# Reordering the start and the last products of an adaLN transformer block: second batch's statistics first, GpSimd held back, sums in pairs, row pairs at the end

## The reference, cut to what matters

```python
mod = (silu(c) @ wmod).reshape(2, 6, 1, 512)          # sa, ca, ga, sb, cb, gb
h = layernorm(x) * (1 + ca) + sa                      # x: (2, 512, 512)
q, k, v = h @ wq, h @ wk, h @ wv                      # 32 query heads, 8 key/value heads of 128
q = q * cos + rotate_half(q) * sin                    # the same for k
att = softmax(where(tril, q @ k.T / sqrt(128), -inf))
x = x + ga * ((att @ v) @ wo)                         # ga, gb: sign kept, size at least 0.25
h = layernorm(x) * (1 + cb) + sb
x12 = h @ w12.T + b12; x1, x2 = split(x12, 2)
x = x + gb * ((silu(x1) * x2) @ w3.T + b3)
```

## Time and profile before

| | us |
|---|---|
| median of 3 runs (795.09 to 797.32) | 795.21 |
| the profiled execution, its own time | 795.66 |
| its span in the profile | 793.9 |

### The profile page before, as it was taken

One profiled execution on the slowest core, in us unless ns is written; L12 is line 12 of the kernel. 1 busy time (PEld: TensorE's weight loads), 2 busy tenths in 40 slices (PEclk: granted clock), 3 DMA queues, 4 the chain that ended last, 5 costly groups with the idle time before them and its releaser, 6 DMA issues.

```text
span 793.9 us, 11522 instructions
## 1 busy us (share of the span) xinstructions
PE 765.9 (96%) x3526; PEld 623.4 (79%) x3526; DVE 604.0 (76%) x1296; ACT 507.3 (64%) x1201; POOL 567.8 (72%) x384
## 2 busy tenths in 40 slices
PE   7999999999999999999999999999999998889997
PEld 2755788887888788887888888888888877667885
DVE  5777878777877787778778786868787788459685
ACT  2466775776676766786677666767677765865331
POOL 2545885879587957795779677898768998447453
PEclk9999999999999999999999999999999999999999
DMA  9625646874867576867776767866677855989011
GB/s 314 232 66 143 204 132 186 193 248 117 238 154 234 157 218 154 219 185 199 182 212 190 192 186 189 251 158 211 145 228 188 280 146 170 272 264 248 1 54 53
DMA packets 189781, 147.13 MB, mean 185 GB/s; under 512 B 60564, under 2 KB 166164, under 8 KB 187672
## 3 DMA queue, kind: packets, MB, share of 16 engines
q1 hardware_dynamic: 189304, 146.33, 65.1%
q10 hardware_dynamic: 416, 0.07, 0.0%
HBM read 91.82 MB, written 54.53 MB: 184 GB/s over the span
## 4 chain that ended last, share of the span: by engine, by line
PE 50%; POOL 22%; DVE 11%; ACT 10%; issue 4%; DMA 3%; SPq 1%; DVEq 0%; ACTq 0%; POOLq 0%
PE q_bank L511 12%; PE out_bank L599 11%; POOL pT_lo L1412 7%; PE o_bank L576 7%; PE x_bank L511 7%; PE s_bank L511 5%; POOL rope_tmp L1438 4%; ACT probs L1185 3%; POOL qT L1412 3%; POOL wo_lo_sb L1412 3%; ACT probs L1193 2%; POOL wq_lo_sb L1412 2%; PE s_bank L798 1%; PE s_bank L785 1%; DVE x_y L1134 1%
## 5 line engine op out<-in xcount | busy, mean ns | idle before, releaser
L1412 POOL TENSOR_TENSOR pT_lo<-pT_raw,pT_hi 128x1024 fp32r<-128x1024 f32 (+1 forms) x96 | 194.2, 2038 | 60.1 <-ACT pT_hi L1162 60.1
L1185 ACT ACTIVATE probs<-probs,neg_max 128x32 f32<-128x32 f32 (+15 forms) x256 | 130.6, 512 | 144.8 <-DVE neg_max L860 144.8
L1412 POOL TENSOR_TENSOR qT<-rope_tmp,qT 128x512 fp32r<-128x512 f32 x64 | 83.7, 1308 | 85.4 <-ACT qT L1162 85.4
L878 DVE STREAM_TRANSPOSE turned<-probs 128x512 f32<-128x512 f32 (+1 forms) x64 | 96.7, 1511 | 36.3 <-DMA spread_dram<-turned 28.3
L1438 POOL TENSOR_TENSOR rope_tmp<-rope_tmp 128x512 f32<-128x512 f32 x80 | 110.4, 1388 | 13.2 <-DVE rope_tmp L825 9.4
L1193 ACT ACTIVATE probs<-probs,row_inv 128x32 f32<-128x32 f32 (+15 forms) x256 | 111.9, 508 | 1.8 <-DVE row_inv L868 1.8
L511 PE MATMUL s_bank<-k_both,qT 128*128 128x416 f32 (+11 forms) x576 | 100.6, 324 | 2.0 <-DVE neg_max L860 2.0
L511 PE MATMUL q_bank<-hT_hi,wq_hi_sb 128*128 128x512 f32 x244 | 97.2, 399 | 5.1 <-DVE rope_tmp L825 5.1
L860 DVE CUSTOM_DVE_ANT_0 probs<-s_bank,mask_sb 128x416 f32<-128x416 f32 (+2 forms) x192 | 87.0, 501 | 15.9 <-PE s_bank L511 15.7
L511 PEld LDWEIGHTS s_bank<-k_both,qT 128*128 128x128 f32 x576 | 90.4, 191 | 9.9 <-DVE neg_max L860 2.6
L599 PE MATMUL out_bank<-wo_hi_sb,attn_hi 128*128 128x512 f32 x248 | 97.0, 391 | 1.2 <-DVE attn_lo L882 1.2
(11 more groups left out here) (267 smaller groups left out, 1673.2 us busy)
## 6 DMA issues: line engine op xcount, KB each, us to landing
spread_dram<-turned SPq DMA_DIRECT2D x64, 256.0 KB, 3.8
pT_raw<-spread_dram SPq DMA_DIRECT2D x16, 1024.0 KB, 5.8
spread_dram<-turned SPq DMA_DIRECT2D x64, 192.0 KB, 4.0
pT_raw<-spread_dram SPq DMA_DIRECT2D x16, 768.0 KB, 4.9
wq_raw<-in_L_attn_wq_dram SPq DMA_DIRECT2D x36, 256.0 KB, 4.2
wo_raw<-in_L_attn_wo_dram SPq DMA_DIRECT2D x9, 1024.0 KB, 5.4
spread_dram<-turned SPq DMA_DIRECT2D x64, 128.0 KB, 4.4
pT_raw<-spread_dram SPq DMA_DIRECT2D x16, 512.0 KB, 5.5
```

The lines of the kernel that those rows point to most:

```text
L878: nc.vector.transpose(dst, src).then_inc(blocks_turned, 1)
L1185: nc.scalar.activation(rows, rows, ACT.Exp, bias=neg_max[:, par, t:t + 1], scale=-1.0, accum_out=row_sum[:, par, t:t + 1]).then_inc(exp_do ...
L1412: nc.gpsimd.tensor_tensor(dst, src, hi.bitcast(f32), ALU.subtract).then_inc(done, 1)
```

## The change

Five edits, all of order or of waits; no instruction is added to or taken from the arithmetic.

1. DVE: the statistics of batch 1 (four `bn_stats` and `norm_scale(1, 2)`) stand ahead of the five first rotations. Before, they stood between them.
2. POOL: the low part of the key weights waits until batch 0 is normalised (`x_normed[0]`), the low parts of query heads 0 and 1 until DVE has made the low parts of `hT` of batch 0 (`h_lo[0]`), those of heads 2 and 3 until `norm_scale` of batch 1 is through (`norm_ready` 2). The low part of the value weights comes after the second query head's rotation.
3. POOL: the sums of the query rotations come in pairs (sum, sum, low, low) instead of one by one.
4. PE and ACT: `modulation_rows(3)` moves up to the place of `project_v(0)`, into bank `s_banks[3]`, and `project_v(0)` moves behind `turn_x(1)`; ACT's copies and high parts are put in the matching order.
5. PE: the last products take rows 0 and 1 through part 2 and part 3 first, then rows 2 and 3.

```diff
-        mod_banks = [q_bank, out_bank, out_bank, q_bank, out_bank, x_bank]
+        mod_banks = [q_bank, out_bank, out_bank, s_banks[3], q_bank, x_bank]
 ...
+                        pe.wait_ge(roped, 5)
                         project_q(out_bank[:, :], 1, 0, h_lo[1])
 ...
+                    if b == 1 and k == KC - 1:
+                        pe.wait_ge(mod_rows_copied, 3)
 ...
             project_q(out_bank[:, :], 0, 1)
-            pe.wait_ge(wv_lo, 1)
-            pe.wait_ge(roped, 1)
-            project_v(0)
+            modulation_rows(3)
 ...
             turn_x(1, range(KC))
+            pe.wait_ge(wv_lo, 1)
+            project_v(0)
             pe.wait_ge(roped, 4)
-            modulation_rows(3)
-            pe.wait_ge(roped, 5)
             modulation_rows(4)
 ...
-            down(1, ([0, 1], [2], [3]))
+            down(1, ([0, 1],))
+            down(1, ([2],), range(2))
+            down(1, ([3],), range(2))
+            down(1, ([2, 3],), range(2, TT))
 ...
-            dve.wait_ge(tables_in, 32)
-            first_rotation(0)
             dve.wait_ge(x_in[2], 16)
             for w in range(TT, 2 * TT):
                 nc.vector.bn_stats(stats[:, w, :], acc[:, w, :]).then_inc(stats_made, 1)
-            first_rotation(1)
             norm_scale(1, 2)
-            first_rotation(2)
-            first_rotation(3)
-            first_rotation(4)
+            dve.wait_ge(tables_in, 32)
+            for n in range(ROPE_FIRST - 1):
+                first_rotation(n)
 ...
+            pool.wait_ge(x_normed[0], TT)
             wk_low(0)
-            for h in range(REP):
-                wq_low(0, h)
-            wv_low(0)
+            pool.wait_ge(h_lo[0], KC)
+            wq_low(0, 0)
+            wq_low(0, 1)
+            pool.wait_ge(norm_ready, 2)
+            wq_low(0, 2)
+            wq_low(0, 3)
             rotated_sum(0, 0)
             rotated_low(0, 0, kT[0][0][:, :], kT[1][0][:, :])
-            pool.wait_ge(norm_ready, 2)
-            for n in range(1, ROPE_FIRST - 1):
+            for n in (1, 3):
                 rotated_sum(0, n)
+                rotated_sum(0, n + 1)
                 q_first(n)
+                q_first(n + 1)
+                if n == 1:
+                    wv_low(0)
```

More of the change, by code:

```diff
@@ L787, in up, with down @@
                     last.then_inc(up_made, 1)
-            def down(b, parts):
+            def down(b, parts, rows=range(TT)):
                 for ms in parts:
@@ L794, in down @@
                         pe.wait_ge(x4_made, 3)
-                    for i in range(TT):
+                    for i in rows:
                         for m in ms:
@@ L1355, in _ @@
             wv_high(0)
-            rotated_high(0, 0, kT[0][0][:, :])
-            rotated_high(0, 1, qT[0][0][:, :, 0, :])
             act.wait_ge(norm_ready, 2)
@@ L1361, in _ @@
                                      scale=rstd[:, w, :]).then_inc(x_normed[1], 1)
-            rotated_high(0, 2, qT[0][0][:, :, 1, :])
+            rotated_high(0, 0, kT[0][0][:, :])
+            copy_rows(3)
+            for h in range(2):
+                rotated_high(0, 1 + h, qT[0][0][:, :, h, :])
             modulate_x(1, 0)
+            rotated_high(0, 3, qT[0][0][:, :, 2, :])
             modulate_x(1, 1)
-            rotated_high(0, 3, qT[0][0][:, :, 2, :])
             modulate_x(1, 2)
+            rotated_high(0, 4, qT[0][0][:, :, 3, :])
             modulate_x(1, 3)
-            rotated_high(0, 4, qT[0][0][:, :, 3, :])
-            copy_rows(3)
             copy_rows(4)
```

## The result

The changed kernel took 791.82 us (median of 5 runs, 790.3 to 792.53), the kernel before 796.07 on the same chip (5 runs, 795.09 to 797.32). The ratio is 0.9944, 95% interval 0.993 to 0.9959: 4.25 us less, with the forecast's 3.65 us (a ratio of 0.9954) inside the interval. The forecast was 791.6.

A forecast was written before the change was run, and what follows sets the result against it. PE, busy 96% of the span, was taken as the bound, leaving its idle time and slow stretches to win. 2.4 (start) + 1.25 (end) = 3.65 us off 795.21 gave 791.6 us, range 789.6 to 793.8.

The forecast's parts named there:

- Part 1: Start: POOL held back from batch 0's normalisation, 1.9 us in place of 4.68; last low parts end at 20.75, not 24.25.
- Part 2: Start: batch 1's statistics first, POOL's new order; first scores about 45.9, 3.8 us sooner; maxima 47.75, 2.4 us sooner.
- the 2.4 us of the sum: Start's share of the forecast gain: DVE begins its maxima 2.4 us sooner, and the rest of the kernel inherits that.
- rival (b): First stall: DVE's lateness has slack, PE's 3.8 us is inherited; 790.2 us; chance 0.16 together with a cheaper clock.
- Part 3: End: new order of last products keeps DVE's last add from meeting POOL's second; gain 1.25 us, bounds 0.4 and 1.4.
- (c): After the start: a later unmoved stall loses the start's gain, only the end's 1.25 us is left; 794.0 us; chance 0.08.
- (d): Start: batch 1's x lands late, holding DVE and the rotations; 2.4 us becomes a 4.45 loss; 798.4 us; chance 0.06.
- (a): First stall: longer PE idle, clock falls again, 793.3 us (chance 0.12); or fall misses PE's work, 789.9 (0.16 with rival (b)).

The follow-up runs named there:

- e3: The kernel before with one wait added: POOL's low part of the key weights waits until batch 0 is normalised; 795.84 us, ratio 0.9999.
- e1: The kernel before with only the new order of the last products, by row pairs; 794.69 us, ratio 0.9983.
- e9: The kernel before with POOL's two waits (normalisation of batch 0, hT's low parts) and the last products by row pairs; 792.95 us, ratio 0.9959.
- e2: The changed kernel with the last products in the old order; 793.07 us, ratio 0.9967 to the kernel before.
- e11: The changed kernel with six more tiny DVE instructions between clearing the strips and the maxima; 792.84 us, ratio 0.9962 to the kernel before.
- e4: The changed kernel with DVE's six strips cleared between the second and third rotation; 791.73 us, ratio 0.9946 to the kernel before.
- e5: The changed kernel without POOL's waits for batch 0's normalisation and hT's low parts; 795.08 us, ratio 0.9986 to the kernel before.
- e7: The changed kernel with DVE's old order (statistics between rotations) and POOL not waiting for the second statistics; 795.77 us, ratio 0.9999 to the kernel before.
- e10: The changed kernel with DVE's old order, POOL not waiting for second statistics, ACT making the key's high part before normalising batch 1; 793.33 us, ratio 0.9969.
- e6: The changed kernel with DVE's old order, statistics of batch 1 between the rotations; 796.76 us, ratio 1.0007 to the kernel before.
- e8: The changed kernel with POOL's query sums one by one, the value weights' low part behind the second; 791.75 us, ratio 0.9943 to the kernel before.

## Why the prediction was right

**Part 1 held in every step.** Normalisation 1.9 us forecast, 1.91 measured. Transposes from 15.2 at full clock: from 15.04, 1.96 us. ACT done at 18.9: 15.79 and 2.78 make 18.57. Low parts done at 20.75: 20.42. The third of a microsecond has three small parts: the tiny transposes ahead came 0.12 sooner in this execution (14.70 for 14.82) and `turn_x(0)` 0.16 in all, ACT followed 0.75 behind instead of 0.78, and its four took 2.78 for 2.92. What Part 1 didn't say is that it needs both waits. It counted the `h_lo` wait as an added wait without effect; e3 shows that without it the whole 3.5 us are lost again in DVE's casts and low parts, but for a few tenths.

**Part 2 had the right numbers, and both of them by luck.** First scores 45.9 forecast and 45.95 measured, although what stood ahead of them came 0.35 to 0.7 us early. The forecast had the last low part wait for ACT's high part, done at 44.5. ACT was done at 43.84, and POOL itself was the last: its last sum and low parts took 1.78 and 3.40 us for the 1.3 and 2.6 that I put in. They stand beside DVE's `h_low`, which I had priced as slowed by POOL without letting it slow POOL in turn. Rotation 4 wasn't hidden either: POOL stood 0.67 us for it ahead of the last sum, and by the forecast's own times the sum at 40.5 should have waited for the rotation's end at 40.95. (The Trainium skill, SBUF — State Buffer, section Who interferes with whom, says that an instruction of VectorE with two SBUF inputs contends with GpSimd's reads, and one with a single SBUF input outside the two-port modes does not. The trace agrees with both halves: `hT_lo`, with two inputs in SBUF, takes 0.69 us alone and up to 1.65 beside POOL, while a rotation, with one input in PSUM, takes 0.65 to 0.70 in the first 95 us of all thirteen traces.) Maxima 47.75 forecast, 47.48 measured, with no wait for scores, as forecast. Here too two errors met: the last `h_low` started 0.64 us sooner than the forecast had it (45.21 for 45.85) and took 1.15 us in place of the 0.7 that I took for it alone.

**The term that was mis-sized** is the 2.4 us of the sum. The maxima moved 2.66, the release 3.06. The difference of 0.4 arises inside the maxima, in their first four instructions: before, they took 1.01 us because PE's scores were still coming in between them, and now they take 0.61. What stands behind them (the kernel before, then the changed one) is already 3.06 us sooner:

```profile
51.07 0.18 DVE L860 CUSTOM_DVE_ANT_0 probs<-s_bank,probs 128x32 f32<-128x32 f32 x1
...
57.11 0.69 DVE L823 TENSOR_TENSOR rope_tmp<-q_bank,cos_sb 128x512 f32<-128x512 f32 x1 [0.24 <-PE q_bank L511]
...
60.38 0.69 DVE L823 TENSOR_TENSOR rope_tmp<-x_bank,cos_sb 128x512 f32<-128x512 f32 x1 [1.18 <-POOL qT L1412]
```

```profile
48.01 0.18 DVE L864 CUSTOM_DVE_ANT_0 probs<-s_bank,probs 128x32 f32<-128x32 f32 x1
...
53.84 0.69 DVE L827 TENSOR_TENSOR rope_tmp<-q_bank,cos_sb 128x512 f32<-128x512 f32 x1
...
57.33 0.69 DVE L827 TENSOR_TENSOR rope_tmp<-x_bank,cos_sb 128x512 f32<-128x512 f32 x1 [1.40 <-POOL qT L1413]
```

The wait of 0.24 us at 57.11 has gone too, but the next rotation waits for POOL that much longer, and nothing of it is left. The other traces agree: from the start of the maxima to the release it is 37.44 to 37.47 us wherever the four instructions take 1.01 (before, e1, e3, e9), and 37.05 to 37.13 in the nine others. So a piece of rival (b) is true, 0.4 of its 1.4 us: the forecast counted PE's lateness only as the wait of 0.47 ahead of the maxima, and missed the 0.4 within them. 3.06 and 1.25 make 4.31, and 4.25 was measured.

**The time came out closer than the gain.** 791.6 was forecast and 791.82 measured, 0.2 us apart, while the gain was 0.6 us larger than forecast. The forecast counted from 795.21, the median of three executions; five have 796.07, and the kernel before has 795.7 to 796.0 in the three sets of 18 to 25. The low base hid the short sum.

**Part 3 held.** 1.25 us forecast; e1 measured 1.24 between medians, and the last add fell from 1.66 to 0.77 us.

**The reason given for Part 2 was wrong, though.** I followed the change's own order, statistics first and then rotations, and got the right times for it. I never worked out what the two waits would do in the old order. They would have given 47.37 for the maxima (e9), as good in the trace as the whole set. The sum was right for the kernel that was built, and told nothing of which edits in it do the work.

**The rivals.** (c), the start's gain lost on the way: e2 keeps 2.86 us of it. (d), a late landing of batch 1's x: the statistics ran at 20.34, with no DMA wait ahead. (b) falls with e11 but for its 0.4 us. (a), the clock: falls of about that size do come and go between executions, but at this stall the changed kernel's trace has none, and they are only a part of the spread (last section).

## What to carry to other kernels

Where DVE's instructions of one shape differ threefold in length, look at what POOL does beside them; hold POOL back until all of DVE's critical stretch is through, since holding it back from a part only moves the collision into the rest (e3: nothing that the time shows, e9: all of it in the trace). When two engines both come sooner, find the one whose lateness the next stall inherits, and delay only that one in an experiment (e11). Several edits that go together aren't several gains: take one at a time into the old kernel, and the smallest set may do what the whole does.

## What the runs showed of the hardware that I had not expected

Behind the first 50 us, and apart from one fall after PE's last work, the clock falls in a few short stretches, and each costs PE the same: the clock lost (1 minus the granted clock, summed over slices of 1 us) is 1.70 to 1.71 us, or twice that, in all thirteen traces. Two of before and the only one of the changed kernel:

```profile
88.00:92.00 4.00, 4.00 (x12) 3.14 (x11) 4.00 (x7) 3.30 (x5) 2.86 (x3) 0.57 0.77 233
699.00:703.00 4.00, 4.00 (x15) 3.81 (x16) 3.29 (x16) 3.76 (x14) 0.00 (x0) 0.57 0.99 236
```

```profile
663.00:667.00 4.00, 3.96 (x10) 3.12 (x11) 4.00 (x14) 2.02 (x3) 3.80 (x2) 0.57 0.22 50
```

and in e9, one of double cost:

```profile
709.00:717.00 8.00, 6.93 (x18) 5.45 (x19) 7.61 (x6) 4.29 (x8) 6.15 (x4) 0.57 0.83 255
```

0.57 over 4 us is half clock for most of it. They come behind one or another of the same few stalls (near 84 to 88, 662, 694 and 708 us), each of them in some traces only. Behind the stall at 84 to 88 us the clock fell in nine traces (before, e1, e3, e4, e5, e7 to e10) and not in four (the changed kernel, e2, e6 and e11). Rival (a) had it that PE's longer idle time at this stall could bring another fall; there the changed kernel has one fewer, and e4, which comes to the same stall 0.4 us sooner, has it. Which executions fall is not settled by anything here.

A stretch doesn't cost the kernel all of it either. Counting from the release to the end of the span, in kernels with the new tail: the changed kernel 703.95 us, e11 703.81 and e6 705.28 with 1.71 us lost behind the release; e1, e5, e7, e8 and e10 705.15 to 705.76 with 3.4 lost; e4 705.74 with 5.1; e9 706.27 with 6.8. One trace of each kernel is not more than a hint, and e6 doesn't fit. The timed executions say more. The mean granted clock is on record for 161 of them, in fifteen sets of one kernel on one chip. Within a set, an execution with a mean clock lower by 0.001, which is 0.8 us of lost clock, is 0.27 us longer. So about a third of the lost clock reaches the end; elsewhere, I take it, PE waits anyway. And the clock accounts for some 36% of the spread within a set. The rest of the 2 or 3 us by which executions of one kernel differ is not explained here. The changed kernel's profiled execution had the highest clock of its five (0.997) and was its shortest.

A second one is the smallest instructions. `norm_scale` is made of instructions on 128x4 elements, most of them 0.16 us long; one that met an instruction of POOL lasted until that was over. In e9, in the middle of that chain:

```profile
29.04 0.16 DVE L1021 TENSOR_TENSOR newton<-rstd 128x4 f32<-128x4 f32 x1
29.23 1.28 DVE L1022 SCALAR_TENSOR_TENSOR newton<-newton,var_eps 128x4 f32<-128x4 f32 x1
```

1.28 us is the length of POOL's instruction beside it (1.29), not of its own 512 elements. In e10 two were met, 0.63 and 1.19 us long, and each ended with POOL's instruction. In these three meetings the price was set by what POOL was doing and not by the size of DVE's instruction.
